# Who gathers a graph layer's rows: from three queues to GpSimd alone, with a wait ahead of each gather

## What is computed

```
h = emb;  acc = emb
for _ in range(2):
    h = segment_sum(adj_val[:, None] * h[adj_col], adj_row, num_segments=N)
    acc = acc + h
graph_item_embs = acc / 3
combined = graph_item_embs[items] + item_features[items]
... attention over the 50 items of a session: tanh, sigmoid, weighted sum -> sess_emb
scores = (12 * l2norm(sess_emb)) @ l2norm(graph_item_embs).T       # 512 x 12501
```

## Time and profile before

| | |
|---|---|
| time, median of 3 runs | 4182.99 us |
| the profiled execution, first to last instruction (the page gives no other time for it) | 6020.2 us |
| VectorE busy | 3014.4 us (50%) |
| GpSimd busy | 2890.1 us (48%) |
| TensorE busy, weight loads beside it | 3070.2 us (51%), 1849.5 us (31%) |
| ScalarE busy | 866.4 us (14%) |
| 16 DMA engines | 39 GB/s over the span |

### The profile page before, as it was taken

One profiled execution on the slowest core, in us unless ns is written; L12 is line 12 of the kernel. 1 busy time (PEld: TensorE's weight loads), 2 busy tenths in 40 slices (PEclk: granted clock), 3 DMA queues, 4 the chain that ended last, 5 costly groups with the idle time before them and its releaser, 6 DMA issues.

```text
span 6020.2 us, 68764 instructions
## 1 busy us (share of the span) xinstructions
PE 3070.2 (51%) x9778; PEld 1849.5 (31%) x9778; DVE 3014.4 (50%) x7257; ACT 866.4 (14%) x3005; POOL 2890.1 (48%) x2965
## 2 busy tenths in 40 slices
PE   5988744444444444444444444444444444445578
PEld 3777622222222222222222222222222222222344
DVE  8999754444444444444444444444444444445455
ACT  2998800000000000000000000000000000000543
POOL 1666654444444444444445454454454454455561
PEclk8888866666666666666666666666666666666689
DMA  0000011111111111111114111111111111112454
GB/s 25 4 3 3 3 48 33 32 31 32 32 31 33 33 34 33 34 33 31 32 32 120 34 37 35 33 37 36 32 37 35 33 37 35 34 36 80 79 84 139
DMA packets 162229, 235.35 MB, mean 39 GB/s; under 512 B 67554, under 2 KB 107776, under 8 KB 161952
## 3 DMA queue, kind: packets, MB, share of 16 engines
q0 software_dynamic: 92896, 171.14, 12.4%
q1 hardware_dynamic: 54132, 58.90, 3.0%
q10 hardware_dynamic: 15052, 3.83, 0.3%
HBM read 192.69 MB, written 41.01 MB: 39 GB/s over the span
## 4 chain that ended last, share of the span: by engine, by line
ACTq 49%; issue 32%; DVE 7%; PE 6%; ACT 3%; another core or an unknown queue 2%; POOL 1%; DMA 0%; DVEq 0%; SPq 0%; POOLq 0%
ACTq L686 43%; ACTq L682 5%; ACT big L644 2%; PE bank L1520 1%; PE bank L1382 1%; POOL sorted_edges L542 1%; DVE stage L944 1%; PE bank L1548 1%; DVE acc L1167 1%; DVE big L888 1%; PE bank L1507 1%; DVE ring L896 0%; PE bank L1482 0%; DVE big L904 0%
## 5 line engine op out<-in xcount | busy, mean ns | idle before, releaser
L1444 PE MATMUL bank<-ring 128*128 128x256 f32 x4976 | 2105.7, 558 | 2135.8 <-DVE ring L1118 1194.1
L1444 PEld LDWEIGHTS bank<-ring 128*128 128x128 f32 x4976 | 1147.7, 263 | 3071.0 <-DVE ring L1118 1662.5
L574 POOL DMA_INDIRECT ring<-in_L_rec_emb,cring x1195 | 1134.9, 950 | 1336.2 <-ACT cring L662 978.9
L1167 DVE TENSOR_TENSOR acc<-acc,bank 128x256 f32 x2488 | 1029.6, 414 | 1481.3 <-remote 1131.6
L1118 DVE TENSOR_SCALAR ring<-bank,mlo,mval 128x256 f32<-128x256 f32 x2488 | 1343.5, 540 | 742.4 <-DMA ring<-in_L_rec_emb 523.1
L574 POOL DMA_INDIRECT ring<-table,cring x1195 | 1130.2, 946 | 1202.8 <-PE bank L1444 795.7
L644 ACT ACTIVATE big<-big 128x68 f32<-128x68 bf16 x1764 | 557.7, 405 | 1.2 <-issue 1.2
L1382 PE MATMUL bank<-big,ring 128*128 128x136 f32 x2352 | 430.8, 328 | 75.5 <-issue 20.8
L542 POOL DMA_INDIRECT sorted_edges<-moved,block_to x313 | 397.2, 1269 | 100.3 <-issue 100.0
L1382 PEld LDWEIGHTS bank<-big,ring 128*128 128x128 f32 x2352 | 356.8, 219 | 147.6 <-ACT big L644 83.2
L660 ACT COPY mlo<-ring 128x24 f32 (+1 forms) x104 | 21.7, 209 | 2415.0 <-issue 2381.6
(11 more groups left out here) (213 smaller groups left out, 1700.7 us busy)
## 6 DMA issues: line engine op xcount, KB each, us to landing
ring<-in_L_rec_emb SPq DMA_DIRECT2D x3136, 0.5 KB
ring<-in_L_rec_emb ACTq DMA_DIRECT2D x3136, 0.5 KB
ring<-table ACTq DMA_DIRECT2D x3136, 0.5 KB
ring<-table SPq DMA_DIRECT2D x3136, 0.5 KB
scores<-stage SPq DMA_DIRECT2D x48, 512.0 KB
ring<-in_L_rec_emb,cring POOLq DMA_INDIRECT x1195
ring<-table,cring POOLq DMA_INDIRECT x1195
table<-big SPq DMA_DIRECT2D x7, 896.0 KB, 9.1
```

The source lines that it names most:

```text
L574: pool.indirect_dma_start(msg[:, s, :], None, source, bass.IndirectOffsetOnAxis(cring[:, s:s + 1], 0)).then_inc(s_g[s], 16)
L1167: add = dve.tensor_tensor(acc[:, bass.ds(off, BUCKET)], acc[:, bass.ds(off, BUCKET)], bank[u % PR][:, 0:BUCKET], ALU.add)
L1444: pe.matmul(bank[u % PR][:, 0:BUCKET], msg[:, h * T + u, :], onehot[:, u % SR, :], start=True, stop=True).then_inc(s_mm[u % M], 1)
```

## The change

GpSimd gathers all 1244 tiles of a layer; `own_rows`, `own_tiles`, the two loads of lines, the three address instructions, the semaphores `s_lines` and `s_line`, and `is_own` go. The wait for an earlier product stands ahead of every gather, and it is for the product 12 tiles back, not 13. One-hots are written six tiles ahead (`LEAD` 4 to 6) and the sums rotate over six banks (`PR` 4 to 6). Bank 5 is one of the six, so the transposed embeddings of layer 1 use bank 6 alone, and TensorE waits for the addition of the stage before (`s_ea` at `c + 2` in place of `c + 1`).

```
-    SR, PR, LEAD = 8, 4, 4
-    PACE, AHEAD = 8, 12
-    LINE = 4 * D
-    HALF, AT_ONCE = P // 2, 32
-    NOWN = NST - 3
+    SR, PR, LEAD = 8, 6, 6
+    AHEAD = 12
...
-    FED = [sum(1 for j in range(u, NU, 2 * T) if not is_own(j)) for u in range(2 * T)]
+    FED = [len(range(u, NU, 2 * T)) for u in range(2 * T)]
...                                                        # SP
-            for half in range(2):
-                sp.dma_start(own_lines[...], lines[...]).then_inc(s_lines, 16)
-            sp.wait_ge(s_mrdy, 3)
-            own_tiles(0, emb_bytes)
...
-            own_tiles(1, table1_bytes)
...                                                        # GpSimd, gather_step
                 for u in range(tiles_of(c)):
                     s = h * T + u
-                    if is_own(T * c + u):
-                        continue
-                    if u % PACE == 0:
-                        done = NU * layer + T * c + u - AHEAD
-                        if done > 0:
-                            pool.wait_ge(s_mm[(done - 1) % M], (done - 1) // M + 1)
+                    done = NU * layer + T * c + u - AHEAD
+                    if done >= 0:
+                        pool.wait_ge(s_mm[done % M], done // M + 1)
                     pool.indirect_dma_start(msg[:, s, :], None, source,
                                             bass.IndirectOffsetOnAxis(cring[:, s:s + 1], 0)).then_inc(s_g[s], 16)
...                                                        # ScalarE: own_rows and its four calls go
                     fetch(0, 2 * i + h, h)
-                    own_rows(emb_bytes, i * (2 * HALF) + HALF * (h - 1), h)
...                                                        # VectorE
-            dve.wait_ge(s_lines, 32)
-            link(dve.tensor_copy(own_at..., own_lines[:, :, :, 0]))
-            link(dve.tensor_single_scalar(own_at, own_at, BUCKET.bit_length() - 1, ALU.arith_shift_right))
-            dve.tensor_single_scalar(own_at, own_at, LINE.bit_length() - 1, ALU.logical_shift_left).then_inc(s_mrdy, 1)
...                                                        # VectorE, one_hot
-                if u % T < T - 1:
-                    dve.wait_ge(s_g[u], 16 * (FED[u] * layer + it + 1))
-                elif isinstance(it, int) and not is_own(2 * T * it + u):
-                    dve.wait_ge(s_g[u], 16 * (FED[u] * layer + (FED[u] if it else 1)))
-                else:
-                    dve.wait_ge(s_line[u // T], 16 * P)
-                    dve.sem_clear(s_line[u // T])
+                dve.wait_ge(s_g[u], 16 * (FED[u] * layer + it + 1))
...                                                        # VectorE, add_embeddings
-                                  bank[5 + h][:, 0:2 * D], ALU.add).then_inc(s_ea, 1)
+                                  bank[6][:, 0:2 * D], ALU.add).then_inc(s_ea, 1)
...                                                        # TensorE, transpose_embeddings
-                pe.wait_ge(s_ea, c + 1)
+                pe.wait_ge(s_ea, c + 2)
                 for q in range(2):
-                    last = pe.transpose(bank[5 + h][:, q * D:(q + 1) * D], gnr[:, h, q, :], ident[:, :])
+                    last = pe.transpose(bank[6][:, q * D:(q + 1) * D], gnr[:, h, q, :], ident[:, :])
```

More of the change, by code:

```diff
@@ L92, in recommender_program @@
     OPEN, NORMS = 5, 8
-    assert NST // 2 - 1 == L // 2 and HALF % AT_ONCE == 0 and NST % 2 == 0
-    assert NT <= N and NST % 2 == 0 and SG % Q == 0 and D == P and 0 < TAIL < P and T % SR == 0 and SR % PR == 0 and LEAD <= PR
+    assert NST % 2 == 0 and SG % Q == 0 and D == P and 0 < TAIL < P and T % SR == 0 and T % PR == 0 and LEAD <= PR <= SR
+    assert NT <= N
     LOOP = 2 * min(NST // 2 - 1, L // 2, NB // 2)
@@ L103, in recommender_program @@
     TC = [T * (NST * n // 3) for n in range(4)]
-    HELD = "a column is held between 0 and N - 1, and an unused slot's is its tile's number, below NT <= N; a line has 512 bytes"
     FITS = "a tile's offset is 256 times the buckets that begin at or before it, less one: 0 to ROWS - 256"
-    def is_own(j):
-        return j % T == T - 1 and 1 <= j // T <= NOWN
-    FED = [sum(1 for j in range(u, NU, 2 * T) if not is_own(j)) for u in range(2 * T)]
+    FED = [len(range(u, NU, 2 * T)) for u in range(2 * T)]
     assert T % 4 == 0 and max(TC[n + 1] - TC[n] for n in range(3)) <= 512
@@ L168, in recommender_program @@
         sorted_rows = big[:, 0:-(-NT // P) * 2 * P].rearrange("p (m s w) -> p m s w", w=2, s=P)
-        at[0] = -(-NT // P) * 2 * P
-        own_lines = carve(big, NOWN * HALF * 2)[0:2, :].rearrange("o (k s w) -> o k s w", k=NOWN, w=2)
-        assert at[0] <= ROWS
         at[0] = 0
@@ L230, in recommender_program @@
         block_at_l = carve(stage, NKL * P)
-        own_at = stage[0:2, 6 * D:6 * D + NOWN * HALF].bitcast(I32)
-        assert 6 * D + NOWN * HALF <= 4 * 512 * 2
         assert at[0] <= 4 * 512 * 2
@@ L340, in recommender_program @@
         s_iota = sem("s_iota")
-        s_lines = sem("s_lines")
-        s_line = [sem(f"s_line{h}") for h in range(2)]
         s_g = [sem(f"s_g{u}") for u in range(2 * T)]
@@ L397, in recommender_program @@
         s_out = [sem(f"s_out{i}") for i in range(4)]
-        emb_bytes = emb.rearrange("n d -> (n d)").bitcast(U8)
-        table1_bytes = table1.rearrange("n d -> (n d)").bitcast(U8)
-        msg_bytes = [msg[:, (h + 1) * T - 1, :].bitcast(U8) for h in range(2)]
         block = ctx.enter_context(nc.Block())
@@ L677, in _ @@
             fetch(0, 1, 1)
[L679 to L690, removed]
             with act.Fori(1, NST // 2 - 1) as i:
@@ L703, in _ @@
                 fetch(1, c, c)
-            act.wait_ge(s_t1w, 16 * (NB // GRP))
-            own_rows(table1_bytes, 0, 1)
             act.wait_ge(s_eld, 32)
@@ L716, in _ @@
                     fetch(1, 2 * i + h + 2, h)
-                    own_rows(table1_bytes, i * (2 * HALF) + HALF * (h + 1), h)
             for c in range(LOOP, max(NB, NST - 2)):
@@ L1103, in _ @@
             decode(T, NT, -(-NT // P))
-            dve.wait_ge(s_lines, 32)
-            link(dve.tensor_copy(own_at.rearrange("o (k s) -> o k s", k=NOWN), own_lines[:, :, :, 0]))
-            link(dve.tensor_single_scalar(own_at, own_at, BUCKET.bit_length() - 1, ALU.arith_shift_right))
-            dve.tensor_single_scalar(own_at, own_at, LINE.bit_length() - 1, ALU.logical_shift_left).then_inc(s_mrdy, 1)
             def one_hot(layer, it, u):
-                if u % T < T - 1:
-                    dve.wait_ge(s_g[u], 16 * (FED[u] * layer + it + 1))
-                elif isinstance(it, int) and not is_own(2 * T * it + u):
-                    dve.wait_ge(s_g[u], 16 * (FED[u] * layer + (FED[u] if it else 1)))
-                else:
-                    dve.wait_ge(s_line[u // T], 16 * P)
-                    dve.sem_clear(s_line[u // T])
+                dve.wait_ge(s_g[u], 16 * (FED[u] * layer + it + 1))
                 dve.tensor_scalar(onehot[:, u % SR, :], bank[7][:, 0:BUCKET], mlo[:, u:u + 1], mval[:, u:u + 1],
```

## The result

| | before | after |
|---|---|---|
| time, median (lowest to highest) | 4183.65 us (4182.49 to 4186.98) | 4306.03 us (4303.48 to 4307.98) |
| ratio of times, 95% interval | | 1.0291 (1.0276 to 1.0305) |
| span of the profiled execution | 6020.2 us | 4301.7 us |

The change makes the kernel 2.9% slower, 122.4 us. The span falls by 1718.5 us in the same comparison, so one of the two profiled executions can't stand for the timed runs. In this part I compare with that second profile.

What follows compares the result with a forecast made beforehand. It took GpSimd's step of 1.25 us per gather as the bound. 4183 + 122.5 - 3.5 + 2 = 4304 us, or 4301 by a 1.223 us step, gave 4303 us; range 4140 to 4380, some 8 in 10.

Steps and rivals of the forecast that it cites:

- 98 gathers at 1.25 us: GpSimd's queue in both layers: 49 more tiles a layer, all on the chain, +122.5 us (119.9 by a 1.223 us step).
- SP's and ScalarE's rows were covered: SP's and ScalarE's queues: 6272 rows fewer each gain nothing, being 25.5 us a stage beside GpSimd's 28.75.
- The first rival: SP's and ScalarE's issues bound the timed run too, so the change is faster: 3615 to 4175 us, chance 0.18.
- The address instructions go, -3.5 us: Start of layer 0: without VectorE's three address instructions, two lengthened gathers shorten by 2.3 + 1.3 us; other end 0.
- A met wait costs 0: GpSimd's queue, ahead of each gather: a wait already met costs 0, upper bound 35 us.
- The wait is always met: GpSimd's queue: 12 tiles ahead give 15 us against 6.3 us from issue to product, so value 0.
- Its far end: GpSimd's waits for products: 7.9 us each if products come as late in a timed run as in layer 1's profile.
- A layer's end, +1.0 us each: VectorE at each layer's end: six additions left after the last tile in place of four, +2 us in all.
- Bank 6 alone, 0: TensorE at the embeddings: waits for the previous stage's addition, some 25 us old; 0, if late under 1 us a stage.
- the 1259 us outside the gathers: Stretches outside the gathers in the first profile, 756.4 + 39.0 + 463.8 us, taken as also present in a timed run.
- Its smaller signs: Changed kernel's profile: first additions under 20 us after a layer's first gather; gathers near 768 us last 0.95 to 1.4 us.
- The rule weighed there: Skill rule that issuing from several engines saves only small issue time; taking SP and ScalarE out would cost nothing.

Runs made afterwards that it cites:

- second profile: The kernel before, profiled once more with no edit: 4184.28 us, span 4182.5 us where its first profiled execution had 6020.2.
- the second experiment: Kernel before with a wait ahead of each gather, six one-hots ahead, six banks, bank 6 alone for embeddings; SP and ScalarE keep their rows: 4190.31 us, ratio 1.000.

## Why the prediction was right

It said 4303 us and the time is 4306.03. The 3 us between are less than runs of one kernel spread over. By its own steps:

1. *98 gathers at 1.25 us.* Right to the size: 1.249 in both kernels, +122.4 us. With 48 more it was 60.1 us. The choice that mattered was to sum on the median with GpSimd's step although the profile showed ScalarE's queue on 43% of the span. It rested on one division, (4183 - 1259) / 104 = 28.1 us a stage against 46 us for ScalarE's rows, and the second profile bears it out.
2. *SP's and ScalarE's rows were covered.* Right: 23.34 us and loads of addresses under a stage of 28.6, and 25.6 us by the experiment that doubled them. The first rival, which had 0.18, needed a step of under 1.175 us; it is 1.249.
3. *The address instructions go, -3.5 us.* Right. In the second profile of before, GpSimd and VectorE at layer 0's start:

```profile
753.68 1.77 DVE L1105 CAST stage<-big 2x3136 int32<-2x3136 f32 x1
755.49 1.78 DVE L1106 TENSOR_SCALAR stage<-stage 2x3136 int32<-2x3136 int32 x1
755.89 3.33 POOL L574 DMA_INDIRECT ring<-in_L_rec_emb,cring  x1 [0.30 <-issue]
```

   Layer 0 there is 4.5 us longer than layer 1, and 1.0 us longer in the changed kernel (the tables above). The difference, 3.5 us, is what was won, in the trace (the prediction's 2.3 and 1.3 are 2.27 and 1.26 before rounding). Two partitions of 3136 numbers delay a gather as the copy of 128 partitions does.
4. *A met wait costs 0.* Right: without them 4307.73 against 4306.03, the halves of the change at 1.000.
5. *The wait is always met.* Right in its verdict, with a term mis-sized. The prediction had 6.3 us from issue to product; the median is 4.35 us, and the step with three tiles ahead gives 4.9 us up to the gather let go. The tail is 8.5 us, which the prediction had no term for. All of these lie under the 15 us of twelve tiles. Its far end, 7.9 us more for products that come late, belonged to that first profile of before alone.
6. *A layer's end, +1.0 us each.* Right for layer 0, too much for layer 1. The last additions of layer 0, once in the second profile of before and once after (they answer):

```profile
2241.51 2.07 DVE L1167 TENSOR_TENSOR acc<-acc,bank 128x256 f32 x4
```

```profile
2298.64 3.17 DVE L1093 TENSOR_TENSOR acc<-acc,bank 128x256 f32 x6
```

   From the last gather of layer 0 to the first of layer 1 it is 2271.7 - 2238.6 = 33.1 us before and 2329.8 - 2295.7 = 34.1 us after. From the last gather of layer 1 to the end of the kernel it is 4182.5 - 3762.7 = 419.8 us before and 4301.7 - 3881.6 = 420.1 after, +0.3 in place of +1.0.
7. *Bank 6 alone, 0.* Not tested by itself; it was in the second experiment, whose ratio is 1.000.

Two things of it did not hold. The span was forecast as 4368 us plus idle times and is 4301.7: the 1259 us outside the gathers are 1195 in every undisturbed profile. The prediction saw that 64 us were too many to close the median, and took the idle times after the layers for the profiler's. They were no part of a timed run, but they came with that one profiled execution, not with profiling as such: the part after the layers, 463.8 us there, is 418.6 in the second. Since the sum went by the median and not by 1259 + 2488 steps, the error did not enter the 4303. And it named L574 as the chain's line in both layers; it is L526 after the edit, and the chain's named pieces cover layer 1 alone, where the gathers are 53% and "issue" 24% of it. Its smaller signs held: the first addition follows the first gather by 17.8 us in layer 0 and 14.4 in layer 1 (it had said under 20), and the gathers at the start of layer 0 last 1.28 us at most.

The rule weighed there, that issuing takes little beside the DMA itself (the Trainium skill, DMA: Bandwidth & Descriptors, section Issuing engines are not separate DMA queues), would have made the change free. Here the rows land a median 2.5 us after the issue, so about two gathers are under way at a time, while the issues follow one another at 1.249 us and set the time. The advice to balance over the engines that can issue (the Trainium skill, Perfetto Trace Analysis; it stands in the section DMA Optimizations, not in the one that the prediction names) agrees with this case: without SP's and ScalarE's share the kernel takes 2.9% more.

No version tried beats the kernel before. SP and ScalarE have under 3 us left of 28.6 in a stage, and at 0.40 us a row that is some seven rows more for each of them by this estimate; I did not try a larger share.

## What to carry to other kernels

When the span of a profile and the timed median are far apart, divide the median by the stages first and ask which engine's undisturbed pace gives that number; profile once more before believing the chain. On an engine whose queue is nothing but DMA issues, count instructions, not bytes: taking one in 24 of them to idle engines was worth 2.9% here, even at the price of 128 single-row DMAs. Size a look-ahead by the latest product at the turn of a stage, not by the median or the mean.

## What the runs showed of the hardware

- An indirect gather on GpSimd has nearly a fixed price: 1.249 us a step for 128 rows of 512 bytes, 1.206 for 64. By these two, about 1.16 us don't depend on the rows (an estimate).
- A VectorE copy from SBUF to SBUF of 1.78 us costs the gathers 1.34 us; four copies out of PSUM, 1.66 us together, cost nothing.
- A single-row DMA from a register address costs SP 0.40 us with its share of an address load when SP issues alone, and about the same when ScalarE issues beside it. ScalarE's 23.34 us for 64 rows and a load of 2.00 us ahead of them are 0.40 us a row too.
- One profiled execution of a kernel can be 44% longer than all others of the same kernel (6020.2 against 4182.5 us), with its ordinary gathers at their usual 1.25 us and SP's and ScalarE's issues up to twice as long.
